# Gathered expert rows of six chunks: added by TensorE into the projection's PSUM group, in place of VectorE

## The reference, cut to what matters

```
logits = x @ w_router.T
_, top_idx = jax.lax.top_k(logits, TOP_K)            # TOP_K = 1
scores = jax.nn.sigmoid(logits) * mask
masked_inputs = scores.T[:, :, None] * x[None, :, :]
gate_up = jnp.einsum('eth,ehf->etf', masked_inputs, gate_up_proj)
gate, up = jnp.split(gate_up, 2, axis=-1)
expert_out = jnp.einsum('etf,efh->eth', up * jax.nn.silu(gate), down_proj)
shared = jax.nn.silu(x @ w_gate.T) * (x @ w_up.T) @ w_down.T
out = shared + expert_out.sum(axis=0)
...
x = _layernorm(x + out)
q = (x @ wq_w + wq_b)      # then k, v; rope on q and k; causal attention
```

## Time and profile before

| | us |
|---|---|
| median of 3 runs (lowest, highest) | 1502.89 (1501.14, 1504.25) |
| span of the profiled execution | 1502.3 |
| TensorE busy | 1372.8 (91%) |
| VectorE busy | 1064.3 (71%) |
| ScalarE busy | 774.2 (52%) |
| GpSimd busy | 321.4 (21%) |

### The profile page before, as it was taken

How to read it: one execution, slowest core, us unless ns; L and a number is a source line. 1 busy time by engine, 2 the same in 40 slices (tenths; PEclk the granted TensorE clock), 3 DMA queues, 4 the chain that set the end, 5 groups by cost and what they waited for, 6 DMA issues and landing times. The chain is left out here.

```text
span 1502.3 us, 24918 instructions
## 1 busy us (share of the span) xinstructions
PE 1372.8 (91%) x9358; PEld 763.0 (51%) x9358; DVE 1064.3 (71%) x2351; ACT 774.2 (52%) x1066; POOL 321.4 (21%) x407
## 2 busy tenths in 40 slices
PE   6898899999999989748998889999999999999996
PEld 3565487857898977413444522333333333333285
DVE  4987466661221238767994788999999999997077
ACT  2344366621111102325774315788888888888754
POOL 3110322242000027633434532000000000000011
PEclk9999899999999999958999868999999999999999
DMA  9548633356888832764430660234322234320001
GB/s 340 189 135 247 167 135 121 126 201 215 284 291 296 280 114 64 215 201 125 130 93 24 185 188 1 67 87 104 74 67 67 74 96 93 69 66 2 1 1 57
DMA packets 153353, 198.69 MB, mean 132 GB/s; under 512 B 16235, under 2 KB 125311, under 8 KB 153106
## 3 DMA queue, kind: packets, MB, share of 16 engines
q1 hardware_dynamic: 141516, 165.34, 36.9%
q0 software_dynamic: 9200, 29.64, 6.4%
q10 hardware_dynamic: 2518, 2.13, 0.4%
HBM read 136.08 MB, written 60.70 MB: 131 GB/s over the span
## 5 line engine op out<-in xcount | busy, mean ns | idle before, releaser
L2134 DVE TENSOR_REDUCE xa_part<-psum 128x1 f32<-128x512 f32 (+1 forms) x768 | 462.7, 662 | 21.2 <-PE psum L1987 19.2
L2086 ACT ACTIVATE xa_P<-psum 128x1024 f32<-128x1024 f32 (+1 forms) x416 | 403.4, 1020 | 103.8 <-PE psum L2011 103.0
L2011 PE MATMUL psum<-sa_Q,xa_K 48*128 48x512 bf16 (+3 forms) x1664 | 267.1, 381 | 4.0 <-DMA sa_Q<-xa_mrow 2.9
L1987 PE MATMUL psum<-xa_K,sa_Q 48*128 48x512 bf16 (+1 forms) x768 | 239.4, 388 | 4.5 <-DVE xa_part L2134 1.5
L2027 PE MATMUL psum<-xa_P,xa_V 128*32 128x512 f32 (+1 forms) x1664 | 222.6, 607 | 0.4 <-ACT xa_P L2086 0.4
L1987 PEld LDWEIGHTS psum<-xa_K,sa_Q 48*128 48x128 bf16 x768 | 59.2, 94 | 232.7 <-DVE xa_part L2134 160.8
L2011 PEld LDWEIGHTS psum<-sa_Q,xa_K 48*128 48x128 bf16 (+3 forms) x1664 | 105.3, 97 | 69.1 <-ACT xa_P L2086 21.2
L2131 DVE CUSTOM_DVE_ANT_0 psum<-psum,cf_sb 128x512 f32<-128x512 f32 (+3 forms) x256 | 119.5, 522 | 27.2 <-PE psum L1987 26.6
L1329 PEld LDWEIGHTS psum<-xtT,wgu 128*128 128x128 f32 x992 | 115.5, 192 | 5.8 <-issue 4.6
L1329 PE MATMUL psum<-xtT,wgu 128*128 128x128 f32 x992 | 115.9, 275 | 1.4 <-issue 0.8
L2086 ACT ACTIVATE sa_P<-psum 128x1024 f32<-128x1024 f32 (+3 forms) x128 | 83.4, 702 | 44.0 <-PE psum L2011 43.9
(11 more groups left out here) (245 smaller groups left out, 2169.3 us busy)
## 6 DMA issues: line engine op xcount, KB each, us to landing
wgu<-in_f_gu SPq DMA_DIRECT2D x31, 1024.0 KB, 6.5
xa_K<-kx SPq DMA_DIRECT2D x192, 100.1 KB, 5.1
wdn<-in_f_dn SPq DMA_DIRECT2D x31, 512.0 KB, 6.9
vx<-xv_v SPq DMA_DIRECT2D x48, 256.0 KB, 3.3
xa_V<-vx POOLq DMA_DIRECT2D x16, 768.0 KB, 6.5
sa_Q<-qs SPq DMA_DIRECT2D x64, 96.0 KB, 2.3
sa_K<-ks SPq DMA_DIRECT2D x64, 96.0 KB, 2.3
sa_Q<-qx SPq DMA_DIRECT2D x64, 96.0 KB, 2.3
```

The costliest lines, as they stand in the source:

```text
L1987: last = pe.matmul(out[:, 0:width], hb.q(u)[tile:tile + HALF, to, qt * P:(qt + 1) * P], hb.k(u)[tile:tile + HALF, to, cut[e]:cut[e] + widt ...
L2011: last = pe.matmul(out(j), hb.k(u)[tile:tile + depth, to, kt * P:kt * P + r], hb.q(u)[tile:tile + depth, to, q0(kt):L], start=(half == 0), ...
L2086: act.activation(Pr[0:r, (u * KT + kt) % PR, h:h + 2, 0:w_], S_PS(p)[0:r, :, 0:w_], ACT.Exp, scale=SCALE).then_inc(s_exp, 1)
L2134: dve.tensor_reduce(part[:, g % 2, col + qt, e:e + 1], src[:, 0:cut[e + 1] - cut[e]], AX, ALU.max).then_inc(s_1free, 1)
```

## The change

For chunks 2 to 7 the two gathered tiles of a chunk are added by TensorE: behind the four products of a tile in PSUM comes a fifth one, with the identity (`env.ident`, part of `cf_sb`) as the stationary operand and the gathered rows as the moving one, in the same accumulation group. The wait for the gather of the chunk (`s_ga[c]`) moves from VectorE to TensorE, ahead of the first of the ten products. VectorE's add (L1622) goes for these chunks and stays for chunks 0 and 1, and its statistics wait for the sum (`s_r`) instead of the add (`s_all`).

```diff
                     if DONE <= c < CHUNKS:
-                        tail.pe_proj(pe, c, lambda k: w["f_wd"][:, k, :],
-                                     lambda i, k: hT[:, k, (2 * c + i) * P:(2 * c + i + 1) * P])
+                        tail.free(pe, tail.s_r, c, tail.slots[1])
+                        pe.wait_ge(s_ga[c], 16 * 2)
+                        for i, t in enumerate(PAIR_TILES(c)):
+                            out = tail.ps(1, c)[:, i * D:(i + 1) * D]
+                            for k in range(FC):
+                                pe.matmul(out, hT[:, k, t * P:(t + 1) * P], w["f_wd"][:, k, :], start=(k == 0), stop=False)
+                            last = pe.matmul(out, env.ident, xs[:, t, :], start=False, stop=True)
+                        last.then_inc(tail.s_proj, 1)
...
                         tail.dve_sum(dve, c, biased=False)
-                        dve.wait_ge(tail.s_r, c + 1)
-                        dve.wait_ge(s_ga[c], 16 * 2)
-                        dve.tensor_tensor(tail.r[:, u, :, :], tail.r[:, u, :, :], xs[:, 2 * c:2 * c + 2, :],
-                                          ALU.add).then_inc(s_all, 1)
-                        tail.dve_stats(dve, c, ready=s_all)
+                        if c < DONE:
+                            dve.wait_ge(tail.s_r, c + 1)
+                            dve.wait_ge(s_ga[c], 16 * 2)
+                            dve.tensor_tensor(tail.r[:, u, :, :], tail.r[:, u, :, :], xs[:, 2 * c:2 * c + 2, :],
+                                              ALU.add).then_inc(s_all, 1)
+                        tail.dve_stats(dve, c, ready=s_all if c < DONE else None)
```

## The result

The changed kernel takes 1511.85 us (median of 4, 1510.85 to 1513.26) against 1503.18 us for the kernel before: ratio 1.0065, 95% interval 1.0052 to 1.0078, slower. The forecast was 1511.3 us. The ratios in this text are those on record, with their intervals; the quotient of the two medians differs from them by up to 0.0007 (1.0058 for the first comparison).

What follows compares the result with a forecast made beforehand. TensorE's unbroken work, then SyncE's run and the barrier, were taken to bound the combining stage. 4.5 + 0.86 - 0.24 + 4 x 0.86 = 8.56, less 0.15, gave 8.4 us on 1502.9: 1511.3 us, range 1506 to 1514 us.

Steps and rivals of the forecast that it cites:

- What bounds the stage: Combining stage: TensorE without pause to step 6's query product, rotation, GpSimd, SyncE's 48.2 us run of transfers, then the barrier.
- Identity products: TensorE, chunks 2 to 7: two products cost 0.86 us a chunk; five chunks on the path (4.3 us), chunk 7 hidden.
- The wait: TensorE ahead of chunk 2's group: waits for the second gather until 563.4 instead of starting at 558.89, costing 4.5 us.
- The clock: TensorE's first group: same loss at the lower granted clock as before, so no change; bounds 1.6 us either way.
- The slack of 0.24 us: After TensorE's first group: transposes had waited for chunk 0's x_sb; now ready long before, giving back 0.24 us.
- VectorE's saving: Six of eight adds go, 4.8 us, mostly becoming waiting; only block 4's store gains, counted as -0.15 us.
- All of it passes to the end: Behind the barrier: the full 8.4 us delay of SyncE's run reaches the end of the kernel.
- A: Rival: TensorE has room, so only the gather wait counts, 4.3 us; 1507.2 us, chance 0.13.
- B: Rival: the delay is caught up after the stage, or SyncE's run shortens; about 1503 to 1505 us, chance 0.07.
- C: Rival: VectorE was the real bound, so the removed adds gain 4.8 us; 1498.1 us, chance 0.05.
- D: Rival: worse than the sum, by a second clock loss of 1.6 us or a 3.7 us gather; 1512.5 to 1514.5 us, chance 0.08.

Runs made afterwards that it cites:

- no_add: Kernel before without VectorE's add of the gathered rows for chunks 2 to 7, nothing in its place; ratio 1.0014 (1.0004 to 1.0024).
- last_only: Kernel before with identity products replacing VectorE's add for chunk 7 alone, gather wait behind its eight products; 1502.48 against 1502.71 us, ratio 1.0000.
- warm_before: Kernel before with 10 unneeded hT products ahead of TensorE's list; 1500.76 us, ratio 0.9995 (0.9986 to 1.0005).
- late_wait: Changed kernel with the gather wait and both identity products moved behind the chunk's eight hT products; 1506.81 against 1502.71 us, ratio 1.0028.
- after_warm: Changed kernel with 20 unneeded hT products ahead of TensorE's list; 1509.85 against 1502.01 us, ratio 1.0049 to the kernel before.
- no_add_again: Kernel before without VectorE's add for chunks 2 to 7, measured in more rounds; ratio 1.0002 (0.9993 to 1.0011).
- changed_again: The changed kernel unaltered, measured in five more rounds against the kernel before; 1513.97 against 1501.88 us, ratio 1.0083.
- wait_only: Kernel before plus TensorE's gather wait ahead of each chunk's eight products, no identity products, VectorE's adds kept; 1508.79 us, ratio 1.0035.
- act_vs: Kernel before with the value stores of three batch elements moved from SyncE's to ScalarE's queue; 1500.03 against 1502.01 us, ratio 0.9984.

## Why the prediction was right, point by point

- **What bounds the stage.** TensorE's time up to the product of step 6, then SyncE's run, then the barrier: right. One sentence went too far: in the kernel before not every VectorE step waited for TensorE. Steps 3 to 6 did (0.54 to 1.91 us at a time), steps 2 and 7 had no pause. Nothing in the sum hung on it. The run moved with TensorE's product in the changed kernel (9.75 and 9.75 us), and did not move when VectorE lost 4.8 us (no_add), TensorE's chunk 7 grew (last_only) or the first group ended early (warm_before, 1.5 us).
- **Identity products, 0.86 us a chunk, five on the path, the sixth hidden.** Right: 4.19 us (late_wait, 4.06 forecast with the slack), the sixth 0.00 (last_only).
- **The wait, 4.5 us.** Right: 4.56 us. The landing was 2.7 us again. The fit of the Trainium skill (DMA: Bandwidth & Descriptors, "Anatomy of one DMA — SWDGE (gpsimd) path") makes it an estimate of 2.3 us; the measurement decides.
- **The clock, no change.** This term was mis-sized. I took the loss of before again (1.6 us), with bounds of 1.6 us to both sides. The group lost 7.08 - 0.86 - 5.05 = 1.17 us more than before, since 5.4 us of it ran at the lower level and not 3.1; with TensorE kept busy ahead of it (after_warm) the whole loss of 2.7 us went. By the sum of the other terms the run was to start 8.56 us late, with this one 9.73 us, and it was 9.75 to 9.81.
- **The slack of 0.24 us.** It fits (the two halves of the change, apart, add up to 0.2 us less than the whole), but is not shown: in other profiles the first group ended up to 0.23 us later and left hardly any of it, with the transposes at the same place (no_add_again: 5.44 us, transposes at 9.90 us from the first gather, as in the kernel before with 9.91).
- **VectorE's saving, 0.15 us.** The gap ahead of block 4 did close, from 0.20 to 0.05 us in the changed kernel, which is the 0.15 us. But this is small beside what runs of stores differ by anyway: the run was 0.42 us shorter.
- **All of it passes to the end.** At the barrier 9.4 us were late; the medians differ by 8.7 and 12.1 us. Nothing was absorbed beyond the scatter of the rest, and the forecast of 8.4 us lay near the first only because the clock's 1.2 us were missing on one side and the medians came out 0.7 us under the barrier's delay on the other. So the closeness of 1511.3 to 1511.85 us is partly luck, and the second comparison's 1513.97 us is only just inside the range to 1514 us.
- **The rivals.** A is refuted by late_wait, B by changed_again, C by both no_add kernels. D was the one that came true in part, by its clock term: 1.17 of 1.6 us. Its times don't quite follow from its terms, which give 1512.9 us for the clock, 1512.3 us for the gather and 1513.9 us for both, not 1512.5 to 1514.5.

## What to carry to other kernels

Work belongs on the engine that waits, and the averages over a kernel don't say which that is: here VectorE is at 71% and TensorE at 91%, but what decides is that in this stage VectorE waited for TensorE in steps 3 to 6, those that lead up to SyncE's run. When an operation moves to another engine its waits move too, and all that follows in that engine's list stands behind them: a wait belongs directly ahead of the operation that needs it, which alone was worth 5.6 of the 9.8 us here (late_wait). Before adding a wait to TensorE, look at whether the granted clock was low there already. Here the wait was paid for twice, with 4.56 us of waiting and 1.2 us more at the lower clock.

## What the runs showed of the hardware

- TensorE's idle time cost more than its length here: after 10.7 to 10.8 us of idle the first group ran 5.3 to 5.5 us at the lower clock (0.50; changed, changed_again, wait_only), after 6.2 us it was 3.1 to 3.5 us (before, late_wait, last_only, no_add_again). Keeping it busy with unneeded products (40 records in 8.87 us) had the group run at the full level, 1.00, from its start: 4.39 instead of 7.08 us (after_warm).
- An identity product that adds a 128x256 f32 tile in PSUM took 0.43 us of TensorE at the full clock, the same as a product of the projection; VectorE's add of two such tiles took 0.69 us.
- SyncE issued more slowly while ScalarE's queue issued too: four loads took 3.07 us beside ScalarE's stores, and 1.86 us alone (act_vs). The same was seen all nine times in three kernels; single groups also took over 1 us longer with SyncE alone (the eight stores of one pair of blocks 6.11 us in before, 5.06 us in the changed kernel), so the cause is likely but not isolated.
- The same program's unchanged 850 us behind the barrier took 848.4 to 853.2 us in 13 profiles.
